# Splitting the last expert weights on GpSimd during the block attention, and starting the experts in its drain

## The reference, cut to what matters

```python
def _moe(h, w_gate, we1, be1, we2, be2):
    x = h.reshape(-1, d)
    raw = jax.nn.softmax(x @ w_gate, axis=-1)
    top_vals, top_idx = jax.lax.top_k(raw, TOP_K)
    w = jax.nn.softmax(top_vals, axis=-1)
    comb = jnp.zeros((t, E), x.dtype).at[jnp.arange(t)[:, None], top_idx].add(w)
    hmid = jax.nn.gelu(jnp.einsum('td,edi->tei', x, we1) + be1[None], approximate=False)
    eout = jnp.einsum('tei,eid->ted', hmid, we2) + be2[None]
    out = jnp.einsum('te,ted->td', comb, eout)
a = _attention(_layernorm(hidden_states, ln1_w, ln1_b), wq, bq, wk, bk, wv, bv, wo, bo)
h = hidden_states + a
m = _moe(_layernorm(h, ln2_w, ln2_b), w_gate, we1, be1, we2, be2)
return h + m
```

## Time and profile before

| | us |
|---|---|
| Median of three runs (range) | 1715.11 (1712.27 to 1715.67) |
| The profiled execution, its own time | 1716.19 |
| Its span in the trace | 1714.8 |
| Last matmul of the attention, start of the last `b_y` additions | 1583.82 |
| First down product of the experts | 1596.98 |
| TensorE, VectorE, ScalarE, GpSimd busy over the span | 1582.6 (92%), 1092.7, 1011.1, 623.4 |

### The profile page before, as it was taken

The page is one execution under the profiler, slowest core; times in us unless marked ns, Lnnn a source line. Parts: engine busy times, 40 slices in busy tenths (PEclk is TensorE's granted clock), DMA queues, the critical chain, the costliest instruction groups (busy, mean ns, idle before and its releaser), DMA issues.

```text
span 1714.8 us, 30308 instructions
## 1 busy us (share of the span) xinstructions
PE 1582.6 (92%) x10908; PEld 1263.0 (74%) x10908; DVE 1092.7 (64%) x2117; ACT 1011.1 (59%) x2041; POOL 623.4 (36%) x537
## 2 busy tenths in 40 slices
PE   5699999699999999999995974999999999999898
PEld 3256564488888888888882543788888888888787
DVE  5788885587545465444445555866877877776554
ACT  4488888354433344333334753877877877776543
POOL 3333332144345433343330152454454464453000
PEclk8699999799999999999995996999999999999899
DMA  7556664343434333333300003345343343431310
GB/s 223 166 183 203 195 199 131 114 131 109 111 114 114 101 114 108 108 108 108 109 23 10 4 3 132 99 153 174 118 147 129 118 140 125 130 118 57 74 50 25
DMA packets 111046, 196.22 MB, mean 114 GB/s; under 512 B 16721, under 2 KB 59541, under 8 KB 108073
## 3 DMA queue, kind: packets, MB, share of 16 engines
q1 hardware_dynamic: 110898, 194.29, 37.0%
HBM read 167.64 MB, written 25.73 MB: 113 GB/s over the span
## 4 chain that ended last, share of the span: by engine, by line
PE 49%; issue 20%; POOL 13%; DVE 7%; ACT 4%; DMA 3%; SPq 2%; POOLq 0%; DVEq 0%; ACTq 0%
POOL e_hidden L1080 12%; PE bank L68 8%; PE bank L69 8%; PE bank L70 8%; PE bank L283 3%; PE bank L321 3%; PE bank L1882 3%; PE bank L1850 3%; PE bank L307 3%; PE bank L1872 1%; PE bank L1366 1%; PE bank L1365 1%; ACT b_turned L1959 1%; PE bank L1376 1%; PE bank L1385 1%
## 5 line engine op out<-in xcount | busy, mean ns | idle before, releaser
L1080 POOL TENSOR_TENSOR e_hidden<-e_gated,e_comb_wide 128x512 f32<-128x512 f32 x132 | 211.3, 1601 | 342.2 <-DVE e_gated L1045 326.6
L917 ACT CAST e_hidden_hi<-e_hidden 128x512 fp32r<-128x512 f32 x132 | 81.9, 621 | 316.7 <-POOL e_hidden L1080 316.7
L1036 DVE TENSOR_TENSOR e_hidden_lo<-e_hidden,e_hidden_hi 128x512 fp32r<-128x512 f32 x132 | 98.2, 744 | 209.9 <-ACT e_hidden_hi L917 209.9
L70 PE MATMUL bank<-e_x_hi,e_weights_lo 128*128 128x512 f32 x520 | 206.2, 397 | 0.0
L68 PE MATMUL bank<-e_x_hi,e_weights_hi 128*128 128x512 f32 x520 | 205.2, 395 | 0.7 <-ACT e_comb_rows L877 0.7
L69 PE MATMUL bank<-e_x_lo,e_weights_hi 128*128 128x512 f32 x520 | 205.2, 395 | 0.0
L1959 ACT ACTIVATE b_turned<-bank,b_swap_bias 64x512 f32<-64x512 f32 x256 | 175.1, 684 | 32.8 <-PE bank L70 28.3
L528 DVE TENSOR_REDUCE a_negmax<-bank 128x2 f32<-128x512 f32 x256 | 164.9, 684 | 34.8 <-PE bank L283 34.0
L2111 POOL TENSOR_TENSOR b_turned<-b_turned,b_rope_q 128x512 f32<-128x512 f32 x64 | 83.5, 1305 | 237.8 <-ACT b_turned L1959 237.8
L424 ACT ACTIVATE a_exp<-bank 128x512 f32<-128x512 f32 x256 | 143.5, 595 | 19.7 <-PE bank L307 11.2
L68 PE MATMUL bank<-e_weights_hi,e_hidden_hi 128*128 128x256 f32 (+1 forms) x528 | 147.7, 280 | 1.7 <-DVE e_hidden_lo L1036 1.7
(11 more groups left out here) (330 smaller groups left out, 4137.5 us busy)
## 6 DMA issues: line engine op xcount, KB each, us to landing
e_comb_wide<-e_combT SPq DMA_DIRECT2D x130, 256.0 KB, 3.9
e_raw<-in_e_weights SPq DMA_DIRECT2D x64, 384.0 KB, 4.4
b_qk_hi<-b_qk_parts SPq DMA_DIRECT2D x64, 256.0 KB, 2.6
b_qk_lo<-b_qk_parts SPq DMA_DIRECT2D x64, 256.0 KB, 2.9
a_qs<-a_q_parts SPq DMA_DIRECT2D x48, 192.0 KB
a_ks<-a_k_parts SPq DMA_DIRECT2D x48, 192.0 KB
b_qk_parts<-columns SPq DMA_DIRECT2D x32, 256.0 KB, 3.5
b_vw_hi<-b_v_parts SPq DMA_DIRECT2D x16, 512.0 KB, 4.0
```

The costliest lines, as they stand in the source:

```text
L70: return pe.matmul(out, w_lo, x_hi, start=False, stop=stop, skip_group_check=True)
L1036: dve.tensor_tensor(lo[rows, :], m.hidden[at % 2][rows, :], hi[rows, :].bitcast(F32), ALU.subtract).then_inc(s.hidden_lo)
L1080: pool.tensor_tensor(m.hidden[i][rows, :], m.gated[i][rows, :], m.comb_wide[u % E_RING][rows, chunk * BANK:(chunk + 1) * BANK], ALU.mult). ...
```

## The change

1. The eight splits move from ScalarE and VectorE at the start of the experts to GpSimd inside the attention: one expert's quarter a step, a copy and a subtraction, in steps 44 to 47 for the up weights and 51 to 54 for the down weights. Their source is a new tile `first_work` (1 MB), in which the attention's input norm has its rows and columns until step 41. SyncE loads the up weights into it at its step 42 (after waiting for the last `x_lo`), and the down weights at its step 49 (after `w_lo` has reached 4).
2. At its step 56, after `w_lo` has reached 8, SyncE loads the four combination rows of chunk 0 into `first_work` too.
3. TensorE makes the up products of expert steps 0 and 1 in the attention's steps 65 and 66, before the projection. ScalarE does their Gelu right behind its last rounding in the attention, before it waits for `y_added`.
4. TensorE no longer waits for `y_added` ahead of the experts but ahead of the first down product, where it also waits for `b2`, which SyncE now loads only after `y_added`, ahead of the combination rows of chunks 1 and 2 (8 DMAs instead of 12).

TensorE, attention step 65 of the kernel before: probabilities turned, values weighed, then at once the projection (12 matmuls, of which three are shown).

The diff, cut to what the text speaks of:

```diff
+EXPERT_LOAD, EXPERT_LAG, EXPERT_NEXT = 2 * RH + INPUT_PIECES, 2, 7
@@ attention_sp
+        if n == EXPERT_LOAD:
+            sp.wait_ge(s.x_lo, NCHUNK)
+            sp.dma_start(m.first_work[:, :, :].rearrange("p e n -> p (e n)"), io["b_w1"]).then_inc(s.experts_in, DMA)
+        if n == EXPERT_LOAD + EXPERT_NEXT:
+            sp.wait_ge(s.w_lo, MOE)
+            sp.dma_start(m.first_work[:, :, :].rearrange("p e n -> p (e n)"), io["b_w2"]).then_inc(s.experts_in, DMA)
+        if n == EXPERT_LOAD + 2 * EXPERT_NEXT:
+            sp.wait_ge(s.w_lo, 2 * MOE)
+            load_moe_comb(k, m.first_work, ring, 0)
...
+def split_expert(k, m, s, i, e):
+    pool = k.nc.gpsimd
+    whole, (high, low) = m.first_work[:, e, :], (t[:, e, :, :].rearrange("p k n -> p (k n)") for t in m.experts[i])
+    pool.wait_ge(s.experts_in, (i + 1) * DMA)
+    pool.tensor_copy(high, whole).then_inc(s.w_hi)
+    pool.wait_ge(s.w_hi, i * MOE + e + 1)
+    pool.tensor_tensor(low, whole, high.bitcast(F32), ALU.subtract).then_inc(s.w_lo)
@@ attention_pe
+        if n > B_STEPS and n - B_STEPS <= EARLY:
+            expert_up(k, m, s, n - B_STEPS - 1)
         if 5 <= n:
             project(n - 5)
@@ attention_pool
+        for i in range(2):
+            if 0 <= n - EXPERT_LOAD - EXPERT_LAG - i * EXPERT_NEXT < MOE:
+                split_expert(k, m, s, i, n - EXPERT_LOAD - EXPERT_LAG - i * EXPERT_NEXT)
+EARLY = 2
@@ moe_sp
     sp.wait_ge(s.y_added, 2 * NCHUNK)
-    for chunk in range(LATE):
-        load_comb(chunk)
+    sp.dma_start(w.b2[:, :], io["b_b2"]).then_inc(s.b2_in, DMA)
+    for chunk in range(1, LATE):
+        load_moe_comb(k, w.combs[chunk - 1], ring, chunk)
@@ expert_up (was up in moe_pe)
+    if n >= 2:
+        pe.wait_ge(s.acted, n - 1)
+    else:
+        pe.wait_ge(s.qk_straight, 2 * B_STEPS)
@@ moe_pe
+        if n == 0:
+            pe.wait_ge(s.y_added, 2 * NCHUNK)
+            pe.wait_ge(s.b2_in, DMA)
         pe.wait_ge(s.hidden_lo, n + 1)
...
-    pe.wait_ge(s.y_added, 2 * NCHUNK)
@@ moe_act
+    act.wait_ge(s.gate_in, 2 * DMA)
+    for n in range(EARLY):
+        activate(n)
     act.wait_ge(s.y_added, 2 * NCHUNK)
-    for e in range(MOE):
-        for i, split in enumerate((w.w1, w.w2)):
-            act.copy(split[0][:, e, :, :], ...).then_inc(s.w_hi)
@@ moe_dve
     dve.wait_ge(s.y_added, 2 * NCHUNK)
-    for e in range(MOE):
-        for i, split in enumerate((w.w1, w.w2)):
-            dve.wait_ge(s.w_hi, 2 * e + i + 1)
-            dve.tensor_tensor(split[1][:, e, :, :], ..., ALU.subtract).then_inc(s.w_lo)
```

More of the change, by code:

```diff
@@ L1667, in store_moe_comb, with load_moe_comb @@
     k.nc.sync.dma_start(k.io["b_comb_rows"][:, cols], m.combT[:, cols]).then_inc(ring["comb_stored"][chunk], DMA)
+def load_moe_comb(k, comb, ring, chunk):
+    k.nc.sync.wait_ge(ring["comb_stored"][chunk], DMA)
+    for e in range(MOE):
+        k.nc.sync.dma_start(comb[:, e, :], k.io["b_comb_rows"][e:e + 1, chunk * BANK:(chunk + 1) * BANK].broadcast_to([P, BANK])).then_inc(ring["comb_in"][chunk], DMA)
+def split_expert(k, m, s, i, e):
[5 more added lines that the diff above has]
+    pool.tensor_tensor(low, whole, high.bitcast(F32), ALU.subtract).then_inc(s.w_lo)
 def gate_pe(k, m, s, chunk, piece, bank, free):
@@ L1684, in gate_pe @@
         pe.wait_ge(s.gate_columns, 2 * chunk + 2)
-        pe.wait_ge(s.gate_in, 3 * DMA)
+        pe.wait_ge(s.gate_in, 2 * DMA)
         pe.wait_ge(*free)
@@ L2187, in down @@
             if e == 0 and mb == 0:
-                pe.matmul(out, m.combT[:, tok], m.b2[:, :], start=t % 2 == 0, stop=False, skip_group_check=True)
-            last = product(pe, out, [v[:, t * P:(t + 1) * P] for v in w.hidden_split[n % 3]], [v[:, e, mb, :] for v in w.w2],
+                pe.matmul(out, m.combT[:, tok], w.b2[:, :], start=t % 2 == 0, stop=False, skip_group_check=True)
+            last = product(pe, out, [v[:, t * P:(t + 1) * P] for v in w.hidden_split[n % 3]], [v[:, e, mb, :] for v in m.experts[1]],
                            False, e == MOE - 1 and mb == MB - 1)
         last.then_inc(s.down_sums)
-    pe.wait_ge(s.y_added, 2 * NCHUNK)
     free = (s.y_added, 2 * NCHUNK)
@@ L2205, in moe_act, with activate @@
     act, banks = k.nc.scalar, k.banks
-    act.wait_ge(s.y_added, 2 * NCHUNK)
-    act.wait_ge(s.experts_in, 2 * DMA)
-    act.wait_ge(s.gate_in, 3 * DMA)
-    for e in range(MOE):
-        for i, split in enumerate((w.w1, w.w2)):
-            act.copy(split[0][:, e, :, :], k.columns[:, i, :].rearrange("p (e k n) -> p e k n", e=MOE, k=DK)[:, e]).then_inc(s.w_hi)
+    def activate(n):
+        (_, e, mb), i = MOE_STEPS[n], n % 2
+        act.wait_ge(s.up_sums, n + 1)
+        if n >= 2:
+            act.wait_ge(s.weighted, n - 1)
+        act.activation(m.acts[i][:, :], banks[i][:, :], ACT.Gelu, bias=m.b1[:, e, mb:mb + 1]).then_inc(s.acted)
+    act.wait_ge(s.gate_in, 2 * DMA)
+    for n in range(EARLY):
+        activate(n)
+    act.wait_ge(s.y_added, 2 * NCHUNK)
     for n in range(len(MOE_STEPS) + MOE_LAG):
@@ L2233, in moe_dve @@
     dve.wait_ge(s.y_added, 2 * NCHUNK)
-    for e in range(MOE):
-        for i, split in enumerate((w.w1, w.w2)):
-            dve.wait_ge(s.w_hi, 2 * e + i + 1)
-            dve.tensor_tensor(split[1][:, e, :, :], k.columns[:, i, :].rearrange("p (e k n) -> p e k n", e=MOE, k=DK)[:, e],
-                              split[0][:, e, :, :].bitcast(F32), ALU.subtract).then_inc(s.w_lo)
     for n in range(len(MOE_STEPS) + MOE_LAG):
@@ L2301, in program @@
         k = Kernel(nc, io, stack)
[L2302 removed]
+        k.resid = stack.enter_context(nc.sbuf_tensor("resid", [P, NB, D], F32))
         k.ident, k.gates = (stack.enter_context(nc.sbuf_tensor(n, s, F32)) for n, s in (("ident", [P, P]), ("gates", [P, 4])))
```

70 lines of the change are left out of this document (31 added, 39 removed).

## The result

The changed kernel takes 1710.09 us (median of 20 runs, 1701.04 to 1720.28), the kernel before in the same comparison 1715.88 (20 runs). The ratio is 0.9965, interval [0.9949, 0.9981]: 0.35% less time, 6 us. A second comparison gave 0.9961 [0.9944, 0.9979]. Single runs of either kernel spread over 15 to 20 us, so what follows rests on the traces, with the timed ratios beside it.

What follows compares the result with a forecast made beforehand. TensorE was taken to bound the attention and to stand idle at the hand-over to the experts. Gain 8.57 minus drain 2.88 gave 5.7 us: 1716.2 to 1710.5, expected median 1709.4 us, range 1703.5 to 1713.5.

Steps and rivals of the forecast that it cites:

- the drain: End of attention: twelve up-product matmuls ahead of the projections of steps 65 and 66 delay it 2.88 us (2.6 to 2.9).
- hand-over: Attention to experts: from the `b_y` additions to the first down product 4.59 instead of 13.16 us, 8.57 less.
- the clock: First down product: TensorE's granted clock falls as before after 3.3 us idle, at the same price, 5.5 us.
- `b2` at 0: Before the first down product: loading `b2` only after `y_added` costs nothing, upper bound 0.6 us.
- The splits on GpSimd: Attention: 1.87 us of GpSimd work in each of eight steps, taken as costing 0; above, 4.5 us.
- the slack of 2.72: Attention step: 2.72 us between the end of VectorE's two additions and the scores needing them; 1.87 us fits in.
- Rival 3, the lock: Attention: each new GpSimd instruction holds VectorE, and TensorE behind it; 15.0 us, 1724.4; 7 in 100 together with a fourth rival.
- Rival 2: Attention: part of the gain is lost to VectorE and SyncE waits; 1712.5 to 1714.9 us; 15 in 100.
- Rival 1: First down product: denser TensorE work before the gap keeps the clock up; another 5.5 us, 1703.9; 13 in 100.
- SyncE, 0: Attention: three 1 MB loads at steps 42, 49 and 56 delay no fetch; cost 0, upper bound 1 us.

Runs made afterwards that it cites:

- the filled gap: Changed kernel plus 12 matmuls of 512 columns, output unread, while TensorE would idle before the first down product; ratio 0.9940 to the kernel before.
- bias rows spread: Kernel before with each chunk's four `b2`-by-combination products moved from the first down group's head to one in every second group; ratio 0.9958 to the kernel before.
- splits in two pieces: Changed kernel with expert weights split by 128x2048 operations in two attention steps, instead of 128x512 in eight; ratio 0.9971 to the kernel before.

## Why the prediction was right

5.7 us less was forecast and 5.8 measured (1715.88 - 1710.09). Some of that closeness is luck: the drain was 1.3 us cheaper than reckoned, a smaller hand-over gain took 0.2 to 0.5 us of that back, the clock, by the chance of the execution, up to 0.7, and the times can't tell the rest from noise.

- **The hand-over, 4.59 us and 8.57 less: right.** 4.76 and 4.75 measured, against 13.16 and 12.84: 8.4 and 8.1 less. The path is the one named, additions, `moe_hidden`, norm pieces, low part, down product. `b2` at 0 was right as well: with it there early the product starts no closer behind its low part, and it holds the product only once the norm pieces are out of the way (hand-over 3.65).
- **The drain, 2.88 us: the term that was mis-sized.** 1.5 and 1.6 measured (16.1 and 16.2 against 14.6). The prediction said that the wait of 1.16 us "isn't cover either", because the last `b_o` is issued only after an earlier projection. It is issued 2.7 us later, as said (9.0 us behind the last scores product before, 11.7 after), but then lands quicker: from issue to the matmul it is 3.9 us before and 2.7 after (1582.61 to 1585.32). That is the whole miss: 2.7 later and 1.2 quicker make the 1.5. It is no accident of one execution: in the nine profiles with up products in the drain it is 2.6 to 2.8 us, in the five without them 3.8 to 4.1, and each time the matmul waited for that transfer to the end. Why it lands quicker no run shows. The wait shrank from 1.16 to 0.44. The lower bound of 2.6 had counted only the short waits.
- **The splits on GpSimd, 0: right, and by the reason given, but not by the prices.** They took more than the earlier trace rows say, beside VectorE (groups by line in the changed kernel from 1410 to 1500: count, busy us, mean ns, idle before), and lengthened the pair of additions; the next block has two such steps in order of time:

```profile
L1694 POOL TENSOR_TENSOR b_expert_lo<-b_first_work,b_expert_hi 128x512 fp32r<-128x512 f32 x8 | 13.0, 1622 | 0.6
...
L1692 POOL CAST b_expert_hi<-b_first_work 128x512 fp32r<-128x512 f32 x8 | 7.7, 962 | 0.0
```
```profile
1416.23 1.84 DVE L2090 TENSOR_TENSOR b_straight<-b_straight,b_turned 128x512 f32<-128x512 f32 x2
1416.45 1.08 POOL L1692 CAST b_expert_hi<-b_first_work 128x512 fp32r<-128x512 f32 x1
...
1417.61 1.62 POOL L1694 TENSOR_TENSOR b_expert_lo<-b_first_work,b_expert_hi 128x512 fp32r<-128x512 f32 x1
...
1419.97 1.05 PE L1877 MATMUL bank<-b_straight 128*128 128x128 f32 x8
...
1431.82 0.61 POOL L1692 CAST b_expert_hi<-b_first_work 128x512 fp32r<-128x512 f32 x1
1431.97 2.71 DVE L2090 TENSOR_TENSOR b_straight<-b_straight,b_turned 128x512 f32<-128x512 f32 x2
1432.52 1.62 POOL L1694 TENSOR_TENSOR b_expert_lo<-b_first_work,b_expert_hi 128x512 fp32r<-128x512 f32 x1
...
1435.59 0.60 PE L1877 MATMUL bank<-b_straight 128*128 128x128 f32 x4
```

 Six of the eight steps are like the first: the cast falls between the two additions, the pair ends at 1418.07 and the scores start at 1419.97, so 1.90 us are left of the slack of 2.72. In the other two the cast is ahead of them and the subtraction falls between: the pair takes 2.71 us, and from its end at 1434.68 to the scores only 0.91 us are left. The waits of the scores for these additions are what they were in the earlier trace rows:

```profile
  DVE b_straight L2090: 3.4, 6
```

- **Rival 3, the lock:** VectorE and GpSimd do hold each other up here. The Trainium skill, page "SBUF — State Buffer", section "Who interferes with whom", says that the later instruction is blocked for the whole of the other. The traces agree: the second addition ends 0.54 us behind the cast in the one kind of step (1417.53, 1418.07) and 0.54 us behind the subtraction in the other (1434.14, 1434.68). It costs VectorE 0.4 us in six steps (1.84 against 1.43) and 1.4 in two (2.71 against 1.28), over 5 us in all. What fails is the rival's next link, TensorE behind VectorE: the slack took up even the 1.4 us, and TensorE lost nothing. Rival 2 fails with it: 505.8 us both times.
- **The clock, the same price: right.** The tail's lost clock is 11.2 and 10.2 before, 12.0 and 10.2 after. Rival 1, that the clock stays up, did not happen; the filled gap shows that its mechanism is real (5.1 us, forecast 5.5) and that up products in the drain do not do it. Its argument that a gap of 2.87 us alone did not bring the clock down holds for one profile only. In the second profile of the kernel before the clock fell right behind that gap, as it did in the one of that kernel with the bias rows spread; the row of the gap and the stretch behind it:

```profile
1586.83 0.73 PE L68 MATMUL bank<-b_x_hi,moe_w_hi 128*128 128x512 f32 x1 [2.87 <-issue]
```
```profile
1587.00:1590.00 3.00, 3.00 (x8) 2.32 (x9) 3.00 (x6) 2.98 (x6) 0.00 (x0) 0.50 0.68 164
```

 The experiments add what the prediction did not see: the larger part of the lost clock hangs on where the four-row products stand.
- **SyncE, 0: right.** No longer wait for a fetch is to be seen in 505.8 us.

Sum by the traces: +1.5 - 8.4 + 0.7 = -6.2 us for the first pair of profiles, +1.6 - 8.1 + 0.0 = -6.5 for the second; by time 5.8 for the first comparison and 6.7 for the second (0.39% of 1716).

## What to carry to other kernels

Look at a hand-over as a race of several waits: taking away all but the longest gives nothing (1.0004), and taking the longest leaves the next (here the router's norm, then `b2`, then the table load), so list their ends before choosing. Read the granted clock behind each idle stretch and behind each run of thin matmuls. Here it cost 10 to 12 us of 118, nearly twice what the change gained, and moving four products per chunk apart recovered 8.5 of it by the traces. Filling the idle time with work that nobody reads brought nothing on top of that.

## What the runs showed of the hardware

- An idle stretch of TensorE of 3.4 us ahead of the first down group: 5.1 us of clock lost in two profiles, 6.8 in a third ("splits in two pieces"); 2.29 us: 5.1; 1.74 us: 3.4; 0.65 us: 1.7; filled: none there. The shorter ones rest on one profile each. With the four-row products spread, the stretch of 3.27 us lost only 1.7.
- Four products of 4 rows by 256 columns, two passes each, among ordinary ones (4.7 us in all) are enough, at full busy share of TensorE, for the clock to fall to 0.50 within or shortly behind them: in 26 cases of 30. With one in every second group it fell in none of 12.
- GpSimd's cast of 128x512 took 1.08 us in the six steps in which it started behind VectorE's first addition and 0.61 in the two in which it started ahead and elsewhere (0.96 on average); the subtraction 1.62 beside the additions and 1.27 elsewhere; as one instruction of 128x2048 they took 2.36 and 4.92, that is 0.59 and 1.23 per 512.
